# Causal attention and a routed feed-forward on one core: the down product in five matmuls over blocks of 128 and 48 columns, and the diagonal minimum ahead of the gating

## What is computed

```
xn  = layernorm(x)
out = x + attention(xn) + ffn(xn)

attention: 16 heads of 16, causal softmax(q k / 4) v, then @ Wo + bo
ffn:       scores = softmax(xn @ gate_w.T); the top 4 of 16 experts, weights made to sum to 1
           y = sum over chosen experts of  w_e * (silu(xn @ w_gate[e]) * (xn @ w_up[e])) @ w_down[e]
           y += (silu(xn @ sw_gate) * (xn @ sw_up)) @ sw_down
```

## Time and profile before

| what | value |
|---|---|
| time, median of three runs | 1192.67 us (1189.87 to 1193.5) |
| the profiled execution's own time | 1192.4 us |
| its span, first to last instruction | 1190.8 us |
| mean granted TensorE clock | 0.935 of full speed |
| PE busy / DVE busy / ACT busy / POOL busy | 84% / 72% / 55% / 49% |

### The profile page before, as it was taken

How to read it: one execution, slowest core, us unless ns; L and a number is a source line. 1 busy time by engine, 2 the same in 40 slices (tenths; PEclk the granted TensorE clock), 3 DMA queues, 4 the chain that set the end, 5 groups by cost and what they waited for, 6 DMA issues and landing times.

```text
span 1190.8 us, 26395 instructions
## 1 busy us (share of the span) xinstructions
PE 1000.6 (84%) x8634; PEld 524.1 (44%) x8634; DVE 862.7 (72%) x1790; ACT 655.0 (55%) x1219; POOL 582.9 (49%) x529
## 2 busy tenths in 40 slices
PE   2877416999989898999998989898989899999875
PEld 1454302444434444544444445444444454444433
DVE  5888787888877767677877766767676767677443
ACT  4777501554535665466666755565656555666431
POOL 6333217777660555356565643565656524644000
PEclk9888755999989999999999999998999999999888
DMA  6998826223232444455454534544454525354602
GB/s 167 280 293 280 247 77 202 62 73 95 70 108 74 96 80 90 78 94 88 94 98 85 99 73 72 99 87 83 74 103 72 110 37 118 62 97 57 137 1 36
DMA packets 99484, 126.41 MB, mean 106 GB/s; under 512 B 24873, under 2 KB 83514, under 8 KB 98834
## 3 DMA queue, kind: packets, MB, share of 16 engines
q0 software_dynamic: 41632, 60.79, 28.4%
q1 hardware_dynamic: 57730, 63.99, 18.3%
HBM read 71.63 MB, written 57.80 MB: 109 GB/s over the span
## 4 chain that ended last, share of the span: by engine, by line
PE 56%; DVE 12%; issue 8%; ACT 4%; DMA 3%; SPq 2%; POOL 0%; ACTq 0%; DVEq 0%
PE gup L1231 12%; PE pvp L1154 11%; PE outs L1258 9%; DVE part L1324 6%; PE smp L1110 6%; PE turn L1243 5%; PE stp L1135 4%; PE outs L1161 4%; PE turn L1201 2%; ACT XC L1511 1%; PE smp L1093 1%; DVE sg L1376 1%; DVE hf L1381 1%; DMA Qs<-nm 1%; ACT th L1500 1%
## 5 line engine op out<-in xcount | busy, mean ns | idle before, releaser
L1494 ACT ACTIVATE probs<-stp 128x1024 f32<-128x1024 f32 (+1 forms) x320 | 300.7, 940 | 281.7 <-PE stp L1135 277.2
L1324 DVE TENSOR_REDUCE part<-smp 128x2 f32<-128x256 f32 (+2 forms) x372 | 345.9, 951 | 44.2 <-PE smp L1093 26.6
L1231 PE MATMUL gup<-gu_w,XC 128*128 (+1 forms) x1152 | 210.4, 319 | 11.7 <-DVE hf L1381 11.4
L952 POOL DMA_INDIRECT XG<-xrow_d,slots x144 | 147.2, 1022 | 80.8 <-issue 40.2
L959 POOL DMA_INDIRECT out<-Y,slots x72 | 117.6, 1633 | 132.8 <-ACT Y L1527 100.9
L1258 PE MATMUL outs<-dn_w,h 88*128 (+1 forms) x1248 | 182.1, 278 | 0.2
L959 POOL DMA_INDIRECT acc_d<-Y,slots x72 | 115.3, 1601 | 121.0 <-ACT Y L1527 98.7
L1154 PE MATMUL pvp<-probs,Vs 128*32 128x512 f32 (+3 forms) x1536 | 166.7, 506 | 1.8 <-DVE probs L1423 1.4
L1376 DVE SCALAR_TENSOR_TENSOR sg<-th,gup 128x176 f32<-128x176 f32 x208 | 70.0, 337 | 129.1 <-ACT th L1500 126.7
L941 POOL DMA_INDIRECT slot_d<-entry,slot_i x128 | 127.3, 995 | 42.9 <-issue 42.9
L1110 PE MATMUL smp<-Ks,Qs 48*128 48x128 f16 (+2 forms) x744 | 112.5, 341 | 42.2 <-DVE part L1324 24.5
(11 more groups left out here) (174 smaller groups left out, 1143.5 us busy)
## 6 DMA issues: line engine op xcount, KB each, us to landing
rb<-rsum_d SPq DMA_DIRECT2D x60, 128.0 KB
Ks<-k_d SPq DMA_DIRECT2D x96, 64.0 KB
Qs<-q_d SPq DMA_DIRECT2D x96, 64.0 KB
v_d<-V SPq DMA_DIRECT2D x8, 544.0 KB, 4.9
Vs<-v_d SPq DMA_DIRECT2D x16, 272.0 KB, 3.2
acc_d<-YA SPq DMA_DIRECT2D x1, 4224.0 KB, 16.8
X<-L_attn_x POOLq DMA_DIRECT2D x8, 512.0 KB, 4.8
xrow_d<-XR SPq DMA_DIRECT2D x8, 512.0 KB, 4.9
```

The lines of the kernel that those rows point to most:

```text
L952: pool.indirect_dma_start(XG[:, q].rearrange("p a c t -> p (a c t)"), None, s.xrow_d, bass.IndirectOffsetOnAxis(ap=slots[:, r, 0:1], axis= ...
L1231: last = pe.matmul(gup[:, 0:2 * I], columns[:, a, h], weights_of(s.gu_w, e, b, h, slice(0, 2 * I)), start=n == 0, stop=n == 5)
L1324: last = dve.tensor_reduce(part[:, g % 2, k0 // CH, :, j, t], banks[:, :, col:col + w], AX.X, ALU.max)
L1494: act.activation(to, of, ACT.Exp, scale=float(DK) ** -0.5 / QS ** 2).then_inc(exp_done, 1)
```

## The change

The down product takes the 176 hidden columns as a block of 128 and a tail of 48 (`IT`). The block of 128 has its three passes. For the tail the weight is laid as one tile `dn_w[:, e, 2]`: rows 0 to 47 the high part, rows 64 to 111 the low part, zeros between; and the high part of the tail's `h16` lies at rows 0 to 47 and again at rows 64 to 111, so that one matmul over 112 rows makes two passes. A fifth makes the last pass.

- PE: `down` has five matmuls instead of six, of 128, 128, 128, 112 and 48 rows instead of 88, all of 256 columns. `turn_h` turns 128 columns twice instead of 88 twice. `down` waits for `hd_done` besides `hl_done`.
- ACT: a new instruction a unit, `tail_again`, copies the high tail (48 x 128, fp16) to rows 64 to 111 of `h16`. It waits for `hl_done`, so for DVE. In a slot with both halves it stands behind `exps` and ahead of `columns` and `gates`; in a slot with a second half alone behind `second_half`.
- DVE: `mask_probs` stands ahead of `silu_times_up` and ahead of the `low_part` of a slot with a second half alone. `low_part` has 128 partitions instead of 88.
- `prepare`: three DMAs instead of one for `w_down` (the tail is loaded twice), and the low part of `dn_w` is two DVE instructions (128 x 256 and 48 x 256) instead of one (88 x 512).

```diff
@@ weights_high, ACT
-                act.wait_ge(gu_in[n], 48 * (done + 1))
+                act.wait_ge(gu_in[n], 80 * (done + 1))
...
@@ load_expert, POOL
-                pool.dma_start(dn[:, n], d.rearrange("(c p) n -> p c n", p=IP)).then_inc(gu_in[n], 16)
+                pool.dma_start(dn[:, n, 0], d[0:P, :]).then_inc(gu_in[n], 16)
+                for r in (0, P // 2):
+                    pool.dma_start(dn[r:r + IT, n, 1], d[P:I, :]).then_inc(gu_in[n], 16)
@@ weights_low, DVE
-                dve.scalar_tensor_tensor(out=dl, in0=dn[:, n], scalar=WS, in1=dh,
+                dve.scalar_tensor_tensor(out=dl, in0=dn[:, n, 0:1], scalar=WS, in1=dh,
+                                         op0=ALU.mult, op1=ALU.subtract).then_inc(lo_made, 1)
+                dve.scalar_tensor_tensor(out=tl[P // 2:P // 2 + IT], in0=dn[P // 2:P // 2 + IT, n, 1:2], scalar=WS,
+                                         in1=tl[P // 2:P // 2 + IT],
                                          op0=ALU.mult, op1=ALU.subtract).then_inc(lo_made, 1)
@@ turn_h, PE
-                    last = pe.transpose(hp[:, c * P:(c + 1) * P], hf[:, v % FB, c * IP:(c + 1) * IP], s.ident[:, :])
+                    last = pe.transpose(hp[:, c * P:(c + 1) * P], hf[:, v % FB, c * P:(c + 1) * P], s.ident[:, :])
@@ down, PE
+            DOWN = ((0, 0, P, 0), (0, 0, P, 1), (1, 0, P, 0), (0, 1, P // 2 + IT, 2), (1, 1, IT, 2))
...
                 pe.wait_ge(hl_done, v + 1)
+                pe.wait_ge(hd_done, v + 1)
...
-                for c in range(2):
-                    for a, b in PASSES:
-                        last = pe.matmul(yp, h16[:, v % 2, a, c], weights_of(s.dn_w, e, b, c, slice(0, D)),
-                                         start=begin and n == 0, stop=end and n == 5)
-                        n += 1
+                for a, c, rows, part in DOWN:
+                    last = pe.matmul(yp, h16[0:rows, v % 2, a, c], weights_of(s.dn_w, e, rows, part, slice(0, D)),
+                                     start=begin and n == 0, stop=end and n == len(DOWN) - 1)
+                    n += 1
@@ the slot loop, DVE
+                    for st in DIAG:
+                        if LAST[st] == n:
+                            mask_probs(g, st)
                     if a is not None:
                         silu_times_up(a)
                     elif z is not None:
                         low_part(z)
                         after_second(z)
-                    for st in DIAG:
-                        if LAST[st] == n:
-                            mask_probs(g, st)
@@ ACT
+            def tail_again(v):
+                act.wait_ge(hl_done, v + 1)
+                act.activation(h16[P // 2:P // 2 + IT, v % 2, 0, 1], h16[0:IT, v % 2, 0, 1], ACT.Copy).then_inc(hd_done, 1)
...
                     exps(g, n)
+                    if a is not None and z is not None:
+                        tail_again(z)
                     if a is not None:
                         if SU <= a + 1 < SU + UT:
                             columns(a + 1 - SU)
                         gates(a)
                     elif z is not None:
                         second_half(z)
+                        tail_again(z)
```

More of the change, by code:

```diff
@@ L57, in token_mixer_with_experts @@
     VW = 4 * (DK + 1)
-    assert D == 256 and N % CH == 0 and I % 2 == 0 and DK == 16
+    assert D == 256 and N % CH == 0 and 0 < IT <= 48 and DK == 16
     nc.disable_value_cache = True
@@ L290, in _ @@
                 pool.memset(t[:, :, :], 0.0)
-            last = pool.memset(s.keepk[:, :], 3.0e38)
+            pool.memset(s.keepk[:, :], 3.0e38)
+            last = pool.memset(dn[:, :, 1], 0.0)
             last.then_inc(const_set, 1)
@@ L345, in expert_parts @@
             return ([one(s.gu_w[:, e, a]).rearrange("p c (a i) -> p c a i", a=2) for a in range(2)],
-                    [one(s.dn_w[:, e, a]) for a in range(2)])
+                    [one(s.dn_w[:, e, 0:3:2])] + [one(s.dn_w[:, e, a:a + 1]) for a in range(3)])
         @block.scalar
@@ L806, in attention_and_experts @@
         xp = turn[:, 0:2 * P].bitcast(F16)
-        hp = turn[0:IP, 2 * P:4 * P]
+        hp = turn[:, 2 * P:4 * P]
         yp = outs[:, 0]
@@ L1182, in spread_sums, with weights_of @@
                 pe.matmul(smp[:, q, :], sel[:, :], rb[:, q], start=True, stop=True).then_inc(spread, 1)
[L1184 removed]
+            def weights_of(t, e, rows, *ix):
                 if isinstance(e, int):
[L1186 to L1187 removed]
+                    return t[(slice(0, rows), e) + ix]
+                return t[(slice(0, rows), bass.ds(e, 1)) + ix].rearrange("p o i -> p (o i)")
+            DOWN = ((0, 0, P, 0), (0, 0, P, 1), (1, 0, P, 0), (0, 1, P // 2 + IT, 2), (1, 1, IT, 2))
             experts = {}
@@ L1230, in gate_up @@
                     for h in range(HC):
-                        last = pe.matmul(gup[:, 0:2 * I], columns[:, a, h], weights_of(s.gu_w, e, b, h, slice(0, 2 * I)),
+                        last = pe.matmul(gup[:, 0:2 * I], columns[:, a, h], weights_of(s.gu_w, e, P, b, h, slice(0, 2 * I)),
                                          start=n == 0, stop=n == 5)
@@ L1380, in silu_times_up @@
                     dve.wait_ge(hT_done, v - FB + 1)
-                dve.scalar_tensor_tensor(out=hf[:, v % FB], in0=sg[:, :], scalar=0.5 * HS / (XS * WS) ** 2,
+                dve.scalar_tensor_tensor(out=hf[:, v % FB, 0:I], in0=sg[:, :], scalar=0.5 * HS / (XS * WS) ** 2,
                                          in1=gup[:, I:2 * I], op0=ALU.mult, op1=ALU.mult).then_inc(hf_done, 1)
```

27 lines of the change are left out of this document (14 added, 13 removed).

## The result

The change makes the kernel slower: 1213.13 us (median of 6 runs, 1210.61 to 1217.82) against 1191.27 us (6 runs, 1185.76 to 1196.69), a ratio of 1.018 with a 95% interval of 1.015 to 1.021, or +22 us (18 to 25). I had forecast 1187, with a range of 1177 to 1202. In what follows a ratio r is given as (r - 1) x 1192 us, so that kernels timed in different series stand side by side.

The account below looks back on a forecast made before the run. PE was taken to set the pace over most of the stretch, with short ACT and DVE turns between. Terms -18 + 4 + 9 + 1 - 5 + 3 = -6 us from 1192.4 gave 1186.4, stated as 1187, range 1177 to 1202.

Parts of the forecast that it names:

- part 3: Tail copy on ACT: mostly hidden, +9 us from 30 places at 0.30 us, +1 us waiting for low_part; down's wait free.
- The rival on the other side: Copy on ACT delays XC, th, sg, hf and the next gup: 75 places at 0.30 us, 1200 us; chance 0.25.
- The bound of +39: Upper bound for the ACT copy: paid in all 130 slots with both halves, +39 us.
- part 1: Down product on PE: one matmul less a unit, 22.8 us of PE, four fifths on the path, -18 us.
- the second rival: PE's saving becomes waiting for DVE's reductions; the matmul brings 10 to 12 us, total 1192 us; chance 0.28.
- part 2: Transposes on PE: load of 128 columns instead of 88, 21 ns longer, one showing a unit, +4 us.
- part 4: Minimum ahead of the gating on DVE: fills idle time before th, which the copy lengthens; -5 us.
- part 5: Prepare: one DVE instruction becomes two, +3 us; the extra DMAs 0; wrong if prepare ends over 5 us later.

Follow-up runs that it names:

- e5: Kernel before plus a copy on ACT that nobody reads, at the change's places, without the wait for DVE: 1221.43 us, ratio 1.028.
- e8: Kernel before plus the unread copy, moved behind columns and gates in slots with both halves, no wait for DVE: 1189.84 us, ratio 0.996.
- e9: Kernel before plus the unread copy only in the 78 slots with a second half alone: 1191.28 us, ratio 0.997.
- e14: Kernel before with Y's scaling on ACT moved behind the gates in slots with both halves and no output projection: 1193.73 us, ratio 1.003.
- e17: Kernel before plus the unread copy, ahead of the exponentials in slots with both halves: 1198.25 us, ratio 1.004.
- e7: The change without the ACT copy and its waits; DVE writes the tail of hf twice instead: 1196.41 us, ratio 1.003.
- e3: The change with the copy moved behind columns and gates in slots with both halves: 1191.94 us, ratio 1.000.
- e16: The change with the copy behind the gates, the w_down tail loaded once, and Y's scaling behind the gates too: 1200.88 us, ratio 1.011.
- e10: Kernel before with one of six down matmuls left out (low x high of the second block): 1183.14 us, ratio 0.9935.
- e11: Kernel before with two of six down matmuls left out (low x high of both blocks): 1174.98 us, ratio 0.985.
- e6: e5 with the unread copy behind the change's wait for DVE's low part: 1224.56 us, ratio 1.0235.
- e1: The change with the diagonal minimum back behind the gating; five matmuls and the copy stay: 1221.7 us, ratio 1.027.
- e2: Kernel before with only the minimum moved ahead of the gating; six matmuls, no copy: 1187.08 us, ratio 0.997.
- e15: e14 with the minimum ahead of the gating besides: 1190.26 us, ratio 1.000.
- e12: Kernel before with prepare's added work alone, two unread DMAs an expert and w_down's low part in two instructions: 1195.42 us, ratio 1.002.

## Why the prediction was wrong

The forecast was a small gain from six terms, -6 us; the change is 22 us slower. Two terms make up most of the 28 us between: the inert copy alone costs 33 us where 10 were forecast, and a matmul alone brings 8 where 18 were. Term by term:

- **The copy on ACT (part 3: +9, and +1 for the wait).** This is the step that failed most. "XC has 1% of the chain ..., some 30 places, so 30 x 0.30": the product, 9 us, was too small by more than three. The inert copy alone costs 33 us (e5), and nothing behind the gates (e8) or in the slots with a second half alone (e9). With 0.43 us a copy that would be some 77 places paid in full, an estimate; the traces do not count them. The count of 30 came from the share of XC in the chain of the one execution before. A chain shows which turn was last, not how close the others were. The rows to read were the idle times in front of the instructions behind the copy. ACT had stood idle in front of XC for 6.2 us in all (in 8 of 144 places), in the kernel before:

```profile
L1511 ACT ACTIVATE XC<-turn 128x512 f16<-128x512 f16 x144 | 85.5, 594 | 6.2 <-PE turn L1201 6.2
```

  So in the other places XC was held by ACT's own work already, and DVE had waited for th in 163 of 208 units. The 277 us of idle time that I set against the copy lie ahead of the exponentials, on their other side (e14, e17). The price was too small as well: the copy of 0.29 us moved XC by 0.43 us.
- **The new wait of down (part 3: "Down needs the copy only a slot later, so its new wait costs nothing").** This step failed too, and the traces show where. PE turns the next unit's `hf` at once and then wants to start `down`, while the copy stands behind DVE's low part on ACT. One such place in the change, a slot with a second half alone:

```profile
711.45 0.41 DVE L1397 TENSOR_TENSOR h<-turn,h 128x256 f16<-128x256 f32 x1
...
711.90 0.31 ACT L1522 ACTIVATE h<-h 48x128 f16<-48x128 f16 x1 [0.68 <-DVE h L1397]
...
711.97 0.41 PE L1254 MATMUL turn<-ident,hf 128*128 128x128 f32 x2 [0.69 <-issue]
...
712.45 0.89 PE L1269 MATMUL outs<-dn_w,h 128*128 x5
```

  The copy ends at 712.21, and the down product starts 0.48 us after the first transpose, where it was 0.26 in the earlier trace rows. In e7, which has the same five matmuls and no copy, it is 0.28:

```profile
708.15 0.44 PE L1254 MATMUL turn<-ident,hf 128*128 128x128 f32 x2
708.43 0.81 PE L1268 MATMUL outs<-dn_w,h 128*128 x5
```

  Taken from the starts in the traces, the distance from the second transpose to the first down matmul is 109 ns in nearly all units before, 24.7 us in sum over the 207 pairs, and 23.8 in e7. In the change it is 37.0 us: in 51 units the copy ends after the second transpose has started, 41 of them with their second half in one of the 78 slots with a second half alone, and these 51 lose 10.6 us; some 36 others lose 4 us for a reason that is open. In e3, with the copy later on ACT, it is 40.9 us and 63 units, in e16 49.0 us and 79 units. So PE gives back over half of the 22.8 us that a matmul a unit is worth. What this costs in the kernel's time was not measured by itself.
- **The rival on the other side** was this very mechanism ("the copy lengthens the gating loop"), with 75 places, about what the estimate above gives, but at 0.30 us, which gave 1200. The bound of +39 stood in part 3, yet the range was closed at 1202 by giving this case 0.25. Its test was a poor one too: I asked for over 60 waits of gup for hf and th above 2% of the chain, and the change shows 36 and under 2%. The delay shows as DVE's wait for th (122.7 us in e8, 161.7 in e5) and reaches PE in several places, each small: the waits for hf, those of the transposes for XC (0.9 us in e8, 8.5 in e5), and those for the reductions (22.3 and 26.1 us).
- **One matmul less (part 1: -18).** On its own it is worth 8 us (e10), two are worth 18 (e11). The share of the path was taken from the chain here as well, 80% where 35 to 40% is right. In the change even that is not seen: from e6 (six matmuls, copy, +28) to e1 (five matmuls, copy, new prepare, +32) it is +4 us with some 8 us of uncertainty, of which prepare is 2 to 3. The pair with the copy behind the gates, which e8 was expected to price, says the same: e8 (six matmuls, minimum last) has -5 and e3 (five, minimum first, new prepare) 0, so no gain can be seen. So the second rival held as well, in part by the waiting that it named (e10, e11) and in part by the wait of down for the copy, which it did not.
- **Wider transposes (part 2: +4).** The load grew by 18 ns where 21 were taken from the slope among transposes. The rule of the Trainium skill ("TensorE: Matmul & The Clock Gate", section "LDWEIGHTS (loading the stationary operand)"), 33 ns for 40 columns, is not what this trace shows. The two transposes start 164 ns apart instead of 147 (medians), 17 ns or 3.5 us of PE in all, near the 4.4 us assumed. The time of this term by itself was not measured.
- **The minimum ahead of the gating (part 4: -5).** Right: -4 us alone (e2), -3 with the scaling moved (e15 against e14), and -10 with the copy (the change against e1). The first two are each near what a comparison can carry; all three point the same way. With the copy there is more idle time ahead of sg for it to fill, 166.6 us in e1 against 119.0 in the change, as part 4 said.
- **Prepare (part 5: +3).** Right in size: +2 (e12, interval -1 to +5). The sign named against it, prepare over 5 us later, is met in the profiled pair: the first gup matmul starts at 202.4 us before and at 207.7 in the change. But that start varies from 202.3 to 204.6 over the twelve kernels with the old prepare (mean 203.5); in the six with the new one it is 204.8 to 208.4 (mean 207.0). So the new prepare is some 3.4 us later, and e12, at 204.2, has only a part of it.

The measured ladder: kernel before 0; inert copy +33 (e5), with its wait +28 (e6); five matmuls and the new prepare +32 (e1); the minimum ahead, +22, the change. That five matmuls bring nothing where leaving one out brings 8 us is explained in part, by PE's wait for the copy and the later prepare. It is not shown to be the whole: no kernel had five matmuls without a wait for a copy and without added work on DVE.

Nothing tried here beats the kernel before by much. e2, the minimum ahead of the gating in the kernel before, is the best complete version at 0.997 (0.994 to 0.9995), 26 us below the change. But e8 and e9, which only add work, measured 0.996 and 0.997, so 0.3% is about what such a comparison can carry, and I would call e2 no worse than the kernel before, not faster.

## What to carry to other kernels

Before an instruction is put into an in-order queue, look at the idle time of that engine directly in front of the next instructions, not at its total: a copy of 0.29 us in 130 slots cost nothing behind the gates, 5 us ahead of the exponentials, and 33 us between them. Then look at who waits for it: a consumer "a slot later" in the program can be on another engine that runs ahead, and then the copy is late. The share of a line in the critical chain of one execution is no measure of what a change to it is worth; here it was too high by two for work taken away (PE) and too low by more than three for time put in (ACT). Where two engines take turns, try an inert copy of the new instruction at its place first: it prices the place with a one-line edit.

## What the runs showed of the hardware

Two things that I had not expected. XC, which reads PSUM, started 0.10 us before the record of the exponentials ahead of it ended, and they read PSUM too; so it is wherever ACT did not wait between them, in the kernel before and in e8. (Not every pair does so: in the earlier trace rows the exponentials start 0.01 us behind Y.) The small copy, from SBUF to SBUF, started 0.03 us after the record ahead of it, and XC 0.02 us after the copy, so that 0.29 us of copy took 0.43 us (e5). A variant with the copy reading PSUM would tell whether the source is the reason; it was not tried, since reads of that bank would have needed further waits.

And the down product of the change, from its first matmul on, saved PE more than a matmul in most units. PE's timeline, first the kernel before, then the change:

```profile
608.78 0.82 PE L1258 MATMUL outs<-dn_w,h 88*128 x6
609.53 0.39 PE L1110 MATMUL smp<-Ks,Qs 48*128 48x128 f16 x4
```
```profile
605.29 0.81 PE L1269 MATMUL outs<-dn_w,h 128*128 x5
605.84 0.49 PE L1117 MATMUL smp<-Ks,Qs 48*128 48x512 f16 x2
```

From the first down matmul to what follows it is here 0.75 us before and 0.55 after. The starts within the five are 109 ns apart up to the one of 112 rows; the one of 48 rows starts 207 ns after that, and its weight load does not start ahead of it as the others do; what follows, also of 48 or 50 rows, starts only 6 or 7 ns later (152 of 208 units), where before it started some 205 ns after the last of 88 rows. Where the next is a matmul of 128 rows (51 units, `values`) the distance is 210 ns, and these units have gained next to nothing. What PE loses ahead of the first down matmul, where it waits for the copy, comes off this gain.
